# Attention scores of a graph kernel: the destination's row by a matmul on the edge tiles' own rows, and no look-ups or gathers of destinations

## The chip, the core and the metric

The kernel runs on 1 core of one Trainium2 chip. The metric is device time in microseconds (us) of one execution. PE is TensorE (PEld its weight load), DVE is VectorE, ACT is ScalarE, POOL is GpSimd, SP is SyncE, which here only issues DMAs.

## What is computed

Two graph blocks over 50,000 nodes of 128 numbers and 25,000 edges sorted by destination, in float32. The first block (ten graph convolutions) gives x1. The second is attention over the edges; the change touches the tables made for both and the scores of the second:

```python
q = (x @ Wq + bq).reshape(n, H, C)
k = (x @ Wk + bk).reshape(n, H, C)
v = (x @ Wv + bv).reshape(n, H, C)
e = (edge_attr @ We).reshape(-1, H, C)
kj = k[src] + e
vj = v[src] + e
alpha = jnp.einsum('ehc,ehc->eh', q[dst], kj) / np.sqrt(C)
```

For every edge this needs the row of x1 of its source (for k and v) and the row of x1 of its destination (for q).

## The kernel before

**Tiles.** The edges fill TE = 196 tiles of 128 (98 pairs of tiles). Odd tiles lie in reverse order. Nodes are placed in slots so that a node with incoming edges has its slot where the run of its edges ends (`lead` is 1 there): its "own" row lies in the same tile and partition as that edge. Other nodes fill the free slots. For every edge tile a 128 x 128 matrix says which edges have the same destination; a matmul with it (`sums_all`) adds up the messages, and `carry` takes a run across a tile's border.

**Stages, in order.** (1) `prepare`: degrees, positions, tables. (2) `local_pass`: all ten layers for nodes without incoming edges, PE bound; beside it DVE builds the same-destination matrices (`build`), POOL looks up tables of positions (`edge_tables`). (3) `coupled_stages`: ten stages over the 98 pairs, first, then (mid, end) four times (r = 0 to 3), last. POOL gathers source rows by indirect DMA. In the end stages of r = 1, 2, 3 POOL also looks up where each destination's row lies (`dst_pair`, 196 indirect DMAs; `found_here`). (4) `scores`, the stage of the change. (5) `shares_and_finish`: softmax, weighted sums, the closing layers, output.

**Scores before.** A pair j takes one of four buffers (s = j % 4) of what is loaded and one of two (s % 2) of most of what is computed. `skewed` writes an engine's program: at turn t it runs each body for pair t minus its lag, in the order of the list; unless `unrolled`, four turns stand in a loop on the engine. POOL (unrolled by a Python loop): four indirect gathers of 128 rows of 512 bytes from x1_tab, two by source, two by destination. SP: three copies of the pair's edge attributes (32 partitions x 1 KB each), and five pairs later the store of the values. PE at turn t: `turn`(t), four transposes into bank s % 2, then `multiply`(t - 1), 14 matmuls of the split (high and low part) product. ACT: `edge_high`(t), `copy`(t) of the transposed rows to their high part, `take`(t - 1) of values and query. DVE: `edge_low`(t), `low`(t), `weigh`(t - 1). The rings that order it: a gather of pair j waits for `turned`(j - 4), a load for `edge_low`(j - 4), `turn`(j) for `low`(j - 2), `take`(j) for the store of pair j - 4.

Of the kernel before, what the change touches and what calls it, by code (L numbers as in the profile page):

```python
# [31 lines left out]
P = 128  # L32
# [173 lines left out]
def gnn_kernel(nc, a, out):  # L206
# [3 lines left out]
    def sb(name, shape, dt=F32):  # L210
        return nc.alloc_sbuf_tensor(name, list(shape), dt)
# [22 lines left out]
    v_tab = dram("v_tab", [SLOTS, D])  # L234
    alpha_line = dram("alpha_line", [HEADS, SLOTS])
# [10 lines left out]
    dst_pair = sb("dst_pair", [P, TE, 2], I32)  # L246
# [11 lines left out]
    with ExitStack() as passing:  # L258
# [6 lines left out]
        early("up", [P, P])  # L265
        early("down", [P, P])
# [14 lines left out]
def prepare(nc, a, S, counts, m):  # L281
# [8 lines left out]
    with ctx:  # L290
        src_i, dst_i, dst_f, up, down, own_three = (m[n] for n in ("src_i", "dst_i", "dst_f", "up", "down", "own_three"))
# [59 lines left out]
        with nc.Block() as block:  # L351
            @block.sync
            def _(sp):
                sp.dma_start(dst_i[:], a["dst"]).then_inc(S["edges_in"], 16)
                sp.dma_start(next_i[:], a["dst_next"]).then_inc(S["edges_in"], 16)
                sp.dma_start(src_i[:], a["src"]).then_inc(S["edges_in"], 16)

            @block.gpsimd
            def _(pool):
                nc.gpsimd.memset(ones[:], 1.0).then_inc(S["filled"], 1)  # L360
# [10 lines left out]
                pool.wait_ge(S["filled"], 2)  # L371
                nc.gpsimd.affine_select(ident[:], ident[:], [[-1, P]], ALU.not_equal, 1.0, base=0,
                                        channel_multiplier=1).then_inc(S["masks"], 1)
                nc.gpsimd.affine_select(up[:], ones[:], [[1, P]], ALU.is_ge, 0.0, base=0,
                                        channel_multiplier=-1).then_inc(S["masks"], 1)
                nc.gpsimd.affine_select(down[:], ones[:], [[-1, P]], ALU.is_ge, 0.0, base=0,
# [3 lines left out]
                nc.gpsimd.memset(m["dst_pair"][:], 0)  # L380
# [8 lines left out]
            def _(dve):  # L389
# [6 lines left out]
                dve.wait_ge(S["masks"], 7)  # L396
# [59 lines left out]
        with nc.Block() as block:  # L456
# [171 lines left out]
            def _(sp):  # L628
                sp.wait_ge(S["rows_set"], 3)
                sp.wait_ge(S["masks"], 8)  # L630
# [5 lines left out]
                sp.wait_ge(S["edges_in"], 96)  # L636


def edge_tables(nc, a, S, m, pool, xo):
# [36 lines left out]
    pool.wait_ge(S["placed"], 32 * TE)  # L676
# [72 lines left out]
def local_pass(nc, a, S, counts, m):  # L749
# [21 lines left out]
    with ctx:  # L771
# [93 lines left out]
        with nc.Block() as block:  # L865
# [196 lines left out]
            def _(dve):  # L1062
# [79 lines left out]
                def build(b, q, odd):  # L1142
# [66 lines left out]
def coupled_stage(nc, S, counts, m, kind, r, source, target, others):  # L1209
# [46 lines left out]
    with nc.Block() as block:  # L1256
# [37 lines left out]
        def _(pool):  # L1294
            def gather(j, s):
# [9 lines left out]
                for t in found_here.get(j, ()):  # L1305
                    pool.indirect_dma_start(
                        out=m["dst_pair"][:, t, :], out_offset=None, in_=m["pos_tab"],
                        in_offset=bass.IndirectOffsetOnAxis(ap=m["dst_i"][:, t:t + 1], axis=0),
                        bounds_check=NPAD - 1, oob_is_err=False).then_inc(S["dst_found"], 16)
# [8 lines left out]
            found_here = {}  # L1318
            if end and r in (1, 2):
                found_here = {j: [(r - 1) * (pairs // 2) + j // 2] for j in range(1, pairs, 2)}  # L1320
            elif end and r == 3:
                found_here = {j: [pairs + j] for j in range(pairs)}
# [302 lines left out]
def scores(nc, a, S, counts, m):  # L1625
# [9 lines left out]
    ph = counts.phase(pairs, {"gathered*": 64, "own_in*": 48, "turned": 1, "copied": 1,  # L1635
# [6 lines left out]
    with ctx:  # L1642
        rows = sb("a_rows", [P, 4, 4, D])

# [18 lines left out]
        with nc.Block() as block:  # L1663
            @block.sync
            def _(sp):
# [25 lines left out]
                skewed(sp, pairs, [(0, load), (5, store)])  # L1691
# [5 lines left out]
            def _(pool):  # L1697
                nc.gpsimd.memset(m["neg_half"][:], -0.5).then_inc(S["a_constants"], 1)

                def gather(j, s):  # L1700
# [3 lines left out]
                    for n, which in enumerate((m["src_pair"], m["dst_pair"])):  # L1704
                        for i in range(2):
                            t = j * 2 + i
                            pool.indirect_dma_start(
                                out=rows[:, s, n * 2 + i, :], out_offset=None, in_=m["x1_tab"],
                                in_offset=bass.IndirectOffsetOnAxis(ap=which[:, t, 0:1], axis=0)
                            ).then_inc(S[f"gathered{s}"], 16)  # L1710
                pool.wait_ge(S["dst_found"], 16 * TE)
# [4 lines left out]
            def _(pe):  # L1716
                pe.wait_ge(S["a_split"], 5)

                def turn(j, s):
# [3 lines left out]
                    for i in range(4):  # L1723
                        last = nc.tensor.transpose(psum[s % 2][:, i * P:(i + 1) * P], rows[:, s, i, :], ident[:])
# [19 lines left out]
                skewed(pe, pairs, [(0, turn), (1, multiply)])  # L1744

            @block.scalar
            def _(act):
# [6 lines left out]
                def edge_high(j, s):  # L1754
                    act.wait_ge(S[f"own_in{s}"], ph.ring_at("own_in", j, s))
                    if past(j, 4):
                        act.wait_ge(S["product"], ph.at("product", j - 4))
                    nc.scalar.activation(edge_parts[0:3 * ED, s, :], edge[:, s, :], ACT.Copy).then_inc(S["edge_high"], 1)

                def take(j, s):  # L1760
# [11 lines left out]
                    last.then_inc(S["query"], 1)  # L1772
                act.wait_ge(S["a_weights"], 288)
                nc.scalar.activation(w_hi[:], m["w_kvq"][:], ACT.Copy).then_inc(S["a_high"], 1)
                nc.scalar.activation(w_edge_hi[:], w_edge[:], ACT.Copy).then_inc(S["a_high"], 1)
                skewed(act, pairs, [(0, edge_high), (0, copy), (1, take)])

            @block.vector
            def _(dve):
# [4 lines left out]
                dve.wait_ge(S["a_split"], 2)  # L1784
                v.tensor_scalar(not_rest[:], is_rest[:], -1.0, 1.0, ALU.mult, ALU.add).then_inc(S["a_split"], 1)
# [578 lines left out]
```

## Time and profile before

| | |
|---|---|
| time of 3 runs | median 7772.25 us (7767.53 to 7774.64) |
| the profiled execution's own time | 7764.07 us, of which 7762.0 us are its span |
| busy in the span | PE 81%, PEld 68%, DVE 78%, ACT 49%, POOL 67% |
| mean granted TensorE clock | 0.925 |
| moved by DMA | 1483 MB in 978,825 packets |

A row of the groups by line has the line, the engine, the operation, output <- inputs, the count, busy time with the mean of one in ns, and the idle time just before with what ended it. Line numbers are those of the kernel before.

### The profile page before, as it was taken

The numbers are of one execution on the slowest core, as the hardware profiler recorded it, in microseconds if no ns is written. First come the engines' busy times: TensorE is split into PE (matmuls) and PEld (weight loads), VectorE is DVE, ScalarE is ACT, GpSimd is POOL, SyncE is SP. The second block draws the span as 40 slices with busy tenths as digits, with TensorE's granted clock in tenths as the row PEclk, the third lists the DMA queues.
The fourth block names the chain that finished last, engine by engine and source line by source line (L and its number), as shares of the span: only waits on it lengthen the run. The fifth ranks groups of instructions, "written<-read, shape, count | busy, mean of one in ns | idle before, by whom it ended". The sixth has DMA issues, their size and how long they took to land. (4 is left out here: it accounts for less than half of the span.)

```text
span 7762.0 us, 157556 instructions
## 1 busy us (share of the span) xinstructions
PE 6300.4 (81%) x37064; PEld 5242.3 (68%) x37064; DVE 6057.8 (78%) x15597; ACT 3773.5 (49%) x10500; POOL 5188.7 (67%) x5858
## 2 busy tenths in 40 slices
PE   7689999999997569899988998899887655557776
PEld 3688898888887348677756776677565545555554
DVE  8678888788887768798888878887898863348887
ACT  6466666666665767435711571157222332234443
POOL 0588888878853768556766676667665656656665
PEclk8899999999998999999999999999999987778998
DMA  0355555554443658797789778977998642224332
GB/s 2 113 162 161 162 164 164 161 159 148 147 155 127 189 182 246 246 302 232 228 296 311 235 226 295 311 234 225 356 388 274 188 141 82 84 88 129 123 122 86
DMA packets 978825, 1483.35 MB, mean 191 GB/s; under 512 B 164277, under 2 KB 445177, under 8 KB 978223
## 3 DMA queue, kind: packets, MB, share of 16 engines
q1 hardware_dynamic: 670639, 909.34, 35.0%
q0 software_dynamic: 153920, 322.36, 15.9%
q10 hardware_dynamic: 153664, 244.12, 8.7%
q8 instruction: 319, 5.23, 0.3%
q14 instruction: 283, 2.32, 0.1%
HBM read 902.55 MB, written 573.01 MB: 190 GB/s over the span
## 5 line engine op out<-in xcount | busy, mean ns | idle before, releaser
L1339 PE MATMUL bank<-c_rows,sums_all 128*128 128x256 f32 (+1 forms) x3920 | 1317.9, 419 | 616.0 <-DVE c_rows L1490 283.5
L743 PE MATMUL bank<-wf_w,c_xt 128*128 128x256 f32 x6272 | 1618.2, 381 | 2.0 <-DVE y L1548 2.0
L1384 ACT ACTIVATE c_xt<-bank 128x512 f32<-128x512 f32 (+1 forms) x980 | 556.1, 567 | 1651.5 <-issue 759.3
L1339 PEld LDWEIGHTS bank<-c_rows,sums_all 128*128 128x128 f32 x3920 | 631.9, 193 | 1056.0 <-issue 499.7
L743 PEld LDWEIGHTS bank<-wf_w,c_xt 128*128 128x128 f32 x6272 | 1135.8, 191 | 127.6 <-ACT c_xt L1384 3.5
L1300 POOL DMA_INDIRECT c_rows<-t_tab,src_pair x784 | 857.7, 1094 | 536.1 <-PE bank L1339 366.5
L1490 DVE SCALAR_TENSOR_TENSOR c_rows<-bank,carry,c_rows 32x256 f32<-32x256 f32 (+1 forms) x1950 | 913.6, 468 | 340.6 <-PE bank L1339 109.6
L1300 POOL DMA_INDIRECT c_rows<-z_tab,src_pair x784 | 768.3, 980 | 291.6 <-issue 189.2
L1022 ACT ACTIVATE lx_hi<-bank 128x512 fp32r<-128x512 f32 (+1 forms) x1000 | 569.8, 572 | 589.1 <-PE bank L991 450.8
L1077 DVE TENSOR_TENSOR lx_lo<-bank,lx_hi 128x512 fp32r<-128x512 f32 (+1 forms) x1000 | 656.8, 657 | 233.0 <-ACT lx_hi L1022 189.8
L733 PE MATMUL bank<-wf_hi,lx_hi 128*128 128x256 f32 x3200 | 724.7, 309 | 76.6 <-issue 51.6
L1504 DVE SCALAR_TENSOR_TENSOR c_u<-bank,lead,c_own 128x256 f32<-128x256 f32 x1764 | 758.4, 467 | 0.4
L733 PE MATMUL bank<-wf_lo,lx_hi 128*128 128x256 f32 x3200 | 658.1, 288 | 0.0
L733 PE MATMUL bank<-wf_hi,lx_lo 128*128 128x256 f32 x3200 | 657.0, 288 | 0.0
L1416 ACT ACTIVATE c_squares<-y,c_root_deg 128x256 f32<-128x256 f32 x980 | 490.0, 501 | 341.6 <-issue 211.3
L1350 PE MATMUL bank<-ident,c_u 128*128 128x128 f32 x3724 | 576.4, 276 | 0.3 <-DVE c_u L1504 0.3
L733 PEld LDWEIGHTS bank<-wf_hi,lx_hi 128*128 128x128 f32 x3200 | 504.3, 196 | 96.7 <-issue 73.0
L1313 POOL TENSOR_TENSOR c_inv<-c_ss,c_neg_half 128x2 f32<-128x2 f32 x588 | 423.5, 720 | 199.6 <-DVE c_ss L1573 89.6
L1999 POOL DMA_INDIRECT out_dram<-fl_y,node_of x396 | 394.9, 997 | 241.8 <-DVE fl_y L2317 145.6
L1350 PEld LDWEIGHTS bank<-ident,c_u 128*128 128x128 f32 x3724 | 473.5, 143 | 93.1 <-issue 3.7
L733 PEld LDWEIGHTS bank<-wf_lo,lx_hi 128*128 128x128 f32 x3200 | 512.1, 196 | 0.0
L733 PEld LDWEIGHTS bank<-wf_hi,lx_lo 128*128 128x128 f32 x3200 | 507.5, 195 | 0.0
(329 smaller groups left out, 14992.6 us busy)
## 6 DMA issues: line engine op xcount, KB each, us to landing
c_z<-z_tab SPq DMA_DIRECT2D x882, 256.0 KB
z_tab<-lz SPq DMA_DIRECT2D x400, 256.0 KB
t_tab<-lt SPq DMA_DIRECT2D x400, 256.0 KB
z_tab<-y ACTq DMA_DIRECT2D x392, 256.0 KB
c_own<-z_tab SPq DMA_DIRECT2D x392, 256.0 KB
t_tab<-y ACTq DMA_DIRECT2D x392, 256.0 KB
c_own<-t_tab SPq DMA_DIRECT2D x392, 256.0 KB
fl_x<-x_tab SPq DMA_DIRECT2D x396, 128.0 KB
```

Source lines behind the costliest of these rows:

```text
L733: last = nc.tensor.matmul(out, x(k), w[:, k, :], start=(n == 0), stop=(n == 3 * ks - 1 and not bias))
L743: last = nc.tensor.matmul(out, x(k), w[:, k, :], start=(k == 0), stop=(k == ks - 1 and not bias))
L1022: nc.scalar.activation(x_hi[:, k].rearrange("p k n -> p (k n)")[:, 0:n], psum[k][:, 0:n], ACT.Copy).then_inc(S["high"], 1)
L1077: v.tensor_tensor(x_lo[:, k].rearrange("p k n -> p (k n)")[:, 0:n], psum[k][:, 0:n], x_hi[:, k].rearrange("p k n -> p (k n)")[:, 0:n].bitc ...
L1300: pool.indirect_dma_start(out=rows[:, s, i, 0:win], out_offset=None, in_=source, in_offset=bass.IndirectOffsetOnAxis(ap=m["src_i"][:, t:t ...
L1313: nc.gpsimd.tensor_tensor(inv[:, s, :], ss[:, s, :], m["c_neg_half"][:], ALU.pow).then_inc(S["inverted"], 1)
L1339: nc.tensor.matmul(psum[s % 2][:, i * win:(i + 1) * win], sums[:, j * 2 + i, :], rows[:, s, i, 0:win], start=True, stop=True).then_inc(S[" ...
L1350: last = nc.tensor.transpose(psum[2 + s % 2][:, k * H2 + i * P:k * H2 + (i + 1) * P], u[:, s % 2, i, k * P:(k + 1) * P], ident[:])
L1384: nc.scalar.activation(xt[:, s % 2].rearrange("p k n -> p (k n)")[:, 0:n], psum[2 + s % 2][:, 0:n], ACT.Copy).then_inc(S["copied"], 1)
L1416: last = nc.scalar.activation(m["c_squares"][:, i, :], y[:, s, i, :], ACT.Square, scale=m["c_root_deg"][:, bass.ds(j * 2 + i, 1)], accum_o ...
L1490: v.scalar_tensor_tensor(rows[p0:p0 + 32, s, i, 0:win], before, m["carry"][p0:p0 + 32, bass.ds(j * 2 + i, 1)], rows[p0:p0 + 32, s, i, 0:wi ...
L1504: last = v.scalar_tensor_tensor(u[:, s % 2, i, 0:win], psum[s % 2][:, i * win:(i + 1) * win], m["lead"][:, bass.ds(j * 2 + i, 1)], u[:, s ...
```

## The change

1. `sums_all` is no longer masked: `build` was a scalar_tensor_tensor with the masks `up` / `down`, and is a tensor_scalar; the two masks go from `prepare`.
2. The 196 look-ups of `dst_pair` in the end stages and the 196 gathers of destination rows in `scores` are dropped.
3. In their place `scores` loads, for each of a pair's two tiles, 127 of the tile's own rows of x1_tab (512 bytes each, every second row of the table) and one row more: of the last edge in the tile's order, from a small table `last_tab`. ACT scales them with `told` (1 where the row is the destination of a run, and at the last edge), and PE multiplies them with `sums_all`: that gives the transposed destination rows directly, two matmuls in place of two transposes.
4. `last_tab` is filled at the start of `scores`: two index loads in `prepare`, two look-ups at the end of `edge_tables`, two gathers, one copy; SP waits for it before its first load.
5. SP and PE are unrolled in `scores`; ACT runs `copy` and `take` one turn later; a load also waits for `turned`(j - 4).

```diff
@@ edge_tables, after the look-ups of the sources
+    for i in range(2):
+        pool.indirect_dma_start(out=m["last_pos"][:, i, :], out_offset=None, in_=m["pos_tab"],
+                                in_offset=at(m["last_dst"][:, i:i + 1]), bounds_check=NPAD - 1, oob_is_err=False
+                                ).then_inc(S["placed"], 16)
@@ local_pass, build
-                    ins = v.scalar_tensor_tensor(built[:, s, i, :], rows_f[:, s, i * P:(i + 1) * P],
-                                                 m["dst_f"][:, bass.ds(b * 8 + (n * 2 + i), 1)],
-                                                 m[("up", "down")[i % 2]][:], ALU.is_equal, ALU.mult)
+                    ins = v.tensor_scalar(built[:, s, i, :], rows_f[:, s, i * P:(i + 1) * P],
+                                          m["dst_f"][:, bass.ds(b * 8 + (n * 2 + i), 1)], None, ALU.is_equal)
@@ coupled_stage, POOL
-                for t in found_here.get(j, ()):
-                    pool.indirect_dma_start(
-                        out=m["dst_pair"][:, t, :], out_offset=None, in_=m["pos_tab"],
@@ scores, SP
+                sp.wait_ge(S["last_found"], 32)
+                sp.dma_start(m["last_tab"], last_rows[0:pairs, :, :]).then_inc(S["last_out"], 16)
+                sp.wait_ge(S["last_out"], 48)
                 def load(j, s):
                     if past(j, 4):
                         sp.wait_ge(S["edge_low"], ph.at("edge_low", j - 4))
+                        sp.wait_ge(S["turned"], ph.at("turned", j - 4))
+                    own = m["x1_tab"].rearrange("(j p i) c -> i p j c", p=P, i=2)
+                    for i, (rows_, row) in enumerate(((slice(0, P - 1), P - 1), (slice(1, P), 0))):
+                        sp.dma_start(ends[rows_, s, i:i + 1, :], own[i][rows_, bass.ds(j, 1), :]
+                                     ).then_inc(S[f"own_in{s}"], 16)
+                        sp.dma_start(ends[row:row + 1, s, i:i + 1, :],
+                                     m["last_tab"].rearrange("j i c -> i j c")[i:i + 1, bass.ds(j, 1), :]
+                                     ).then_inc(S[f"own_in{s}"], 16)
-                skewed(sp, pairs, [(0, load), (5, store)])
+                skewed(sp, pairs, [(0, load), (5, store)], unrolled=True)
@@ scores, POOL: two gathers a pair by src_pair in place of four; before them
+                for i in range(2):
+                    pool.indirect_dma_start(
+                        out=last_rows[:, i, :], out_offset=None, in_=m["x1_tab"],
+                        in_offset=bass.IndirectOffsetOnAxis(ap=m["last_pos"][:, i, 0:1], axis=0)
+                    ).then_inc(S["last_found"], 16)
@@ scores, PE, turn
-                    for i in range(4):
-                        last = nc.tensor.transpose(psum[s % 2][:, i * P:(i + 1) * P], rows[:, s, i, :], ident[:])
+                    for i in range(2):
+                        nc.tensor.transpose(psum[s % 2][:, i * P:(i + 1) * P], rows[:, s, i, :], ident[:])
+                    pe.wait_ge(S["edge_high"], ph.at("edge_high", j))
+                    for i in range(2):
+                        last = nc.tensor.matmul(psum[s % 2][:, (2 + i) * P:(3 + i) * P], ends[:, s, i, :],
+                                                m["sums_all"][:, j * 2 + i, :], start=True, stop=True)
-                skewed(pe, pairs, [(0, turn), (1, multiply)])
+                skewed(pe, pairs, [(0, turn), (1, multiply)], unrolled=True)
@@ scores, ACT, edge_high, and the order of the bodies
+                    for i in range(2):
+                        nc.scalar.activation(ends[:, s, i, :], ends[:, s, i, :], ACT.Copy,
+                                             scale=told[:, bass.ds(j * 2 + i, 1)])
-                skewed(act, pairs, [(0, edge_high), (0, copy), (1, take)])
+                skewed(act, pairs, [(0, edge_high), (1, copy), (2, take)])
```

## Rows read from the trace of the kernel before

**Rows 1.** Windows: end stages of r = 0, 1 and 3, then the scores.

```profile
core 0: us, PE busy (x) PEld busy (x) DVE busy (x) ACT busy (x) POOL busy (x), PEclk, DMA share, GB/s
...
3175.00:3550.00 375.00, 336.77 (x1571) 247.90 (x1571) 335.17 (x786) 109.54 (x197) 191.89 (x203) 0.96 0.87 281
...
3885.00:4330.00 445.00, 375.90 (x1675) 268.09 (x1676) 365.67 (x790) 58.53 (x98) 287.00 (x256) 0.96 0.89 296
...
5435.00:5915.00 480.00, 409.51 (x1755) 283.58 (x1755) 445.82 (x873) 109.01 (x196) 309.87 (x290) 0.97 1.02 372
...
6350.00:6944.00 594.00, 335.11 (x1764) 323.99 (x1764) 206.34 (x600) 149.44 (x590) 374.43 (x393) 0.71 0.28 82
```

**Rows 2.** Groups by line and form in the stretch of the scores.

```profile
L1707 POOL DMA_INDIRECT a_rows<-x_tab,dst_pair x196 | 188.9, 964 | 59.7 <-issue 59.7
L1707 POOL DMA_INDIRECT a_rows<-x_tab,src_pair x196 | 185.4, 946 | 144.0 <-remote 81.3 <-issue 45.7 <-PE bank L1724 16.8
...
L1724 PE MATMUL bank<-ident,a_rows 128*128 128x128 f32 x392 | 82.3, 348 | 25.8 <-DVE a_w_edge_parts L1798 24.6 <-issue 0.6 <-DMA a_rows<-x_tab,dst_pair 0.6
...
L1770 ACT ACTIVATE a_q<-bank 128x128 f32<-128x128 f32 x196 | 45.3, 299 | 0.0
```

**Rows 3.** ACT's timeline in the scores: two starts after idle time (start, us).

```profile
6592.11 0.45 ACT L1765 ACTIVATE a_v<-bank 128x128 f32<-128x128 f32 x2 [9.65 <-remote]
6603.85 0.45 ACT L1765 ACTIVATE a_v<-bank 128x128 f32<-128x128 f32 x2 [8.74 <-remote]
```

**Rows 4.** Waits in 6400 to 6900 us, summed: us, times, longest.

```profile
ACT a_v L1765 <- remote: 308.5, 35, 10.8
```

**Rows 5.** DMA queues in 231 to 234 us: packets, MB, share of 16 engines.

```profile
q1 hardware_dynamic: 675, 0.67, 71.3%
```

**Rows 6.** SP's timeline just before: three copies of 99 partitions each.

```profile
229.42 0.36 SPq L632 DMA_DIRECT2D pos_tab<-pos_rows  x1
...
230.26 1.02 SPq L634 DMA_DIRECT2D own_tab<-late_rows  x1
```

**Rows 7.** DMA queues in 2500 to 2800 us (first coupled stage).

```profile
q1 hardware_dynamic: 47585, 22.94, 26.8%
```

**Rows 8.** DMA queues in 6400 to 6900 us (scores).

```profile
q0 software_dynamic: 10848, 22.24, 15.3%
q1 hardware_dynamic: 24048, 19.16, 12.7%
```

**Rows 9.** SP's timeline where its program is unrolled (last stage).

```profile
7199.85 0.43 SPq L1974 DMA_DIRECT2D fl_x<-x_tab  x1
7200.32 0.43 SPq L1968 DMA_DIRECT2D fl_x<-x_tab  x1
```

**Rows 10.** PE in the first coupled stage, by form: matmul with `sums_all`.

```profile
L1339 PE MATMUL bank<-c_rows,sums_all 128*128 128x128 f32 x392 | 98.4, 334 | 151.8 <-DVE c_rows L1490 123.0 <-issue 28.7
```

**Rows 11.** Timeline at the start of the scores.

```profile
6351.32 1.02 POOL L1707 DMA_INDIRECT a_rows<-x_tab,src_pair  x1 [0.60 <-issue]
...
6358.40 7.14 SPq L1685 DMA_DIRECT2D a_edge<-in_edge_attr  x14
...
6361.38 0.42 ACT L1758 ACTIVATE a_edge_parts<-a_edge 96x256 fp32r<-96x256 f32 x1 [0.26 <-DMA a_edge<-in_edge_attr]
```

**Rows 12.** SP's timeline at the end of the scores.

```profile
6926.19 1.24 SPq L1685 DMA_DIRECT2D a_edge<-in_edge_attr  x3
```

**Rows 13.** The look-ups: ns min/median/max, first and last start.

```profile
L1306 POOL DMA_INDIRECT dst_pair<-pos_tab,dst_i x196: 1002/1007/1213, 3889.4 to 5891.7; - x196
```

**Rows 14.** Waits in 5440 to 5910 us (end stage of r = 3).

```profile
POOL c_rows L1300 <- PE bank L1339: 82.6, 88, 2.1
```

**Rows 15.** `lbuilt` in the local pass: ns min/median/max.

```profile
L1158 DVE SCALAR_TENSOR_TENSOR lbuilt<-lrows_i,dst_f,up x98: 319/344/364, 253.7 to 2351.1; 128x128 f32<-128x128 f32 x98
```

**Rows 16.** Window in the local pass, columns as in rows 1.

```profile
300.00:2200.00 1900.00, 1727.15 (x13749) 1678.03 (x13750) 1531.47 (x2995) 1245.23 (x3623) 1523.03 (x1982) 0.95 0.53 158
```

**Rows 17.** Timeline of the kernel's first microseconds: DVE's first work.

```profile
5.53 1.21 DVE L398 CAST dst_f<-dst_i 128x196 f32<-128x196 int32 x1 [5.53 <-POOL above L378]
```

More of the change, by code:

```diff
@@ L234, in gnn_kernel @@
     v_tab = dram("v_tab", [SLOTS, D])
+    last_tab = dram("last_tab", [TE // 2, 2, D])
     alpha_line = dram("alpha_line", [HEADS, SLOTS])
@@ L356, in _ @@
                 sp.dma_start(src_i[:], a["src"]).then_inc(S["edges_in"], 16)
+                sp.wait_ge(S["filled"], 1)
+                for i, row in enumerate((P - 1, 0)):
+                    sp.dma_start(m["last_dst"][0:TE // 2, i:i + 1],
+                                 a["dst"][row:row + 1, :].rearrange("o (j i) -> i j o", i=2)[i],
+                                 allow_slow_non_contiguous=True).then_inc(S["last_out"], 16)
             @block.gpsimd
             def _(pool):
+                nc.gpsimd.memset(m["last_dst"][:], 0).then_inc(S["filled"], 1)
                 nc.gpsimd.memset(ones[:], 1.0).then_inc(S["filled"], 1)
@@ L1317, in _ @@
                 pool.wait_ge(S["c_constants"], 1)
[L1318 to L1322, printed above, removed]
             for j in range(pairs + (8 if rooted else 0)):
@@ L1634, in scores @@
     v, psum, ident = nc.vector, m["psum"], m["ident"]
-    ph = counts.phase(pairs, {"gathered*": 64, "own_in*": 48, "turned": 1, "copied": 1,
+    ph = counts.phase(pairs, {"gathered*": 32, "own_in*": 112, "turned": 1, "copied": 1,
                               "product": 1, "query": 1, "values": 1, "weighed": 1, "alpha": 1, "stored*": 16,
@@ L1642, in scores @@
     with ctx:
-        rows = sb("a_rows", [P, 4, 4, D])
+        rows = sb("a_rows", [P, 4, 2, D])
+        ends = sb("a_ends", [P, 4, 2, D])
+        last_rows = sb("a_last_rows", [P, 2, D])
+        told = sb("a_told", [P, TE])
         K = 3 * ED + 2
@@ L1703, in gather @@
                         pool_wait(pool, S[f"gathered{s}"], ph.ring_at("gathered", j, s, back=1), S["apart"])
[L1704 to L1711, printed above, removed]
+                    for i in range(2):
+                        t = j * 2 + i
+                        pool.indirect_dma_start(
+                            out=rows[:, s, i, :], out_offset=None, in_=m["x1_tab"],
+                            in_offset=bass.IndirectOffsetOnAxis(ap=m["src_pair"][:, t, 0:1], axis=0)
+                        ).then_inc(S[f"gathered{s}"], 16)
+                for i in range(2):
+                    pool.indirect_dma_start(
+                        out=last_rows[:, i, :], out_offset=None, in_=m["x1_tab"],
+                        in_offset=bass.IndirectOffsetOnAxis(ap=m["last_pos"][:, i, 0:1], axis=0)
+                    ).then_inc(S["last_found"], 16)
                 for j in range(pairs):
@@ L1755, in edge_high @@
                     act.wait_ge(S[f"own_in{s}"], ph.ring_at("own_in", j, s))
+                    for i in range(2):
+                        nc.scalar.activation(ends[:, s, i, :], ends[:, s, i, :], ACT.Copy,
+                                             scale=told[:, bass.ds(j * 2 + i, 1)])
                     if past(j, 4):
@@ L1784, in _ @@
                 dve.wait_ge(S["a_split"], 2)
+                for i, row in enumerate((P - 1, 0)):
+                    v.tensor_scalar(told[:].rearrange("p (j i) -> p j i", i=2)[:, :, i],
+                                    m["lead"][:].rearrange("p (j i) -> p j i", i=2)[:, :, i],
+                                    ident[:, row:row + 1], None, ALU.max)
                 v.tensor_scalar(not_rest[:], is_rest[:], -1.0, 1.0, ALU.mult, ALU.add).then_inc(S["a_split"], 1)
```

26 lines of the change are left out of this document (11 added, 15 removed).

## The prediction

> **What bounds the kernel now.** I read the table of windows by stage first, since the kernel is a row of stages with different limits, and then only the stages that the change touches. In the end stages DVE is busy 82 to 93% of the time and PE 84 to 90%, and the DMA engines up to 1.02 of their time, above one because services on an engine overlap a little [rows 1]. The scores are another world: 594 us for 98 pairs, 6.06 us a pair, with PE busy 56%, POOL 63%, DVE 35%, the clock at 0.71 and the DMA engines at 0.28 [rows 1]. No engine is full.
>
> The groups by line say why POOL is not: 392 gathers of 0.95 us with 0.3 us between them are 5.0 us a pair, and it stands 81 us for something that is not an engine's recorded end [rows 2]. ACT's timeline shows the beat: it starts once in 12 us, after 9 to 10 us of idle time, and then does two pairs at once [rows 3]; 35 such waits are 308 of 500 us [rows 4]. So the stage goes in steps of two pairs: PE does two products, ACT, DVE and PE wait for one another through rings of two, and POOL's gathers hang on `turned` of four pairs back. The profile doesn't name the cause of the long waits; any load that takes under about 6 us a pair is hidden in that beat, and one that takes more becomes the bound.
>
> **The loads of own rows.** This is the term that decides. A pair gets two copies of 127 partitions with one run of 512 bytes each, on SP's queue. The question is on how many of the 16 DMA engines such a copy runs. The nearest rows are three copies of 99 partitions, issued within 0.9 us with nothing beside them [rows 6]: while they run, 16 engines are busy 71.3% [rows 5], that is 11.4 engines; 99 is 9 x 11, and 11 of 16 would be 69%, where 15 engines (seven rows each) would be 94%. So the copy was dealt out in equal shares to the largest number of engines that divides its partitions. 127 is a prime number. By that reading (an estimate: no copy of a prime number of rows is in the trace) all 127 rows go to one engine, for both copies of every pair.
>
> The Trainium skill, page "DMA: Bandwidth & Descriptors", section "Why a DMA increments its semaphore by 16 and not by 1", says that for a DMA from SP or ACT the count of engines is the largest one up to 16 that divides the slowest dimension of both sides, gives 127 partitions as a case of one engine, and puts it on the lowest-numbered engines; the row of 99 agrees with it (11 engines), no row shows 127. It also tells of an exception, for some copies from POOL, where 127 partitions are shared out over all 16; by that the stage would be the first rival below, some 7600 us for the kernel; by the rule for SP it is the sum that follows.
>
> Price of a row: in the first coupled stage SP's queue moves almost only 512-byte runs: 47,585 packets and 22.94 MB in 300 us at 26.8% of 16 engines [rows 7], 0.268 x 300 x 16 / 47,585 = 27.0 ns a packet; if the few 4-byte packets in it cost nothing, 22.94 MB are 44,800 rows of 28.7 ns. I take 28 ns. Two copies are 254 rows x 28 ns = 7.11 us a pair on one engine.
>
> That engine has its share of the rest too. In 500 us (82.5 pairs) of the scores SP's queue took 12.7% of every engine and POOL's 15.3% [rows 8]: 0.77 us a pair for edges and stores, which stay, and 0.93 us for four gathers, of which half stay, 0.46 us. The two single rows and semaphore writes are some 0.04 us. Sum: 7.11 + 0.77 + 0.46 + 0.04 = 8.38 us a pair. The other 15 engines have 1.3 us.
>
> Is this engine kept fed? Loads run up to four pairs ahead (they wait for `turned` and `edge_low` of j - 4), and the store of j - 5, behind which the next load is queued on SP, waits for values that ACT writes one load's landing later. So two to three loads, 16 to 25 us of its work, lie in the ring while ACT, PE, ACT, DVE and PE pass a pair on in less; even a late beat of 12 us is covered. Stores stand in the same ring, but `take` wants that of four pairs back, which lands with load j + 5 and before the load that ACT awaits anyway. PE's new wait, for `edge_high`(j) and so for load j, has `multiply`(j - 1) behind it: product, values and store of a pair come one load later, which the rings allow. So the engine sets the pace.
>
> **The rest of the scores** lies under 8.38 us a pair. SP: eight issues of 0.47 us when unrolled [rows 9], 3.8 us. POOL: two gathers, 2.5 us. PE: two transposes of 348 ns [rows 2] become two matmuls of 334 ns [rows 10], nothing to 0.1 us on 3.4 us (335 us / 98). ACT: two scalings of 0.30 us, priced by `a_q` of the same size [rows 2], 0.6 on 1.5 us. The unrolling costs instruction loads and takes away loop branches; both lie beside the engine's work. If the engine were not the bound, SP's 3.8 us and PE's 3.4 to 3.8 us would be next.
>
> **Start and end of the stage.** The first load was issued at 6358.4, after 18 weight copies; its data were used at 6361.38 [rows 11]. POOL starts its gathers at 6351.32, so the two gathers of last rows are done when SP comes to `last_tab`; its copy and the wait for it cost one such landing, 2.5 to 3 us. The engine starts at about 6361. The last edges were issued at 6926.2 to 6927.4 [rows 12] and the stage ended at 6944, 17 us later; of that I put 14 us behind the last landing. Stage end: 6361 + 98 x 8.38 (821) + 14 = 7196, against 6944: +252 us. Overlap of services, at least the 2% of the 1.02 row, takes off 16 us: +236.
>
> **The parts outside.** The look-ups: 196 x 1.3 us of POOL's time [rows 13], but in the stage that has the most of them (r = 3, 98) POOL stood 83 us for PE in 88 waits [rows 14], so they are hidden; the work they were hidden by is the chain of DVE and PE through `carried`. Their small packets, where the engines are full, may be worth 4 us. Bounds: 0 and, if every look-up delayed a gather on the chain, all 255 us, which POOL's waits for PE exclude; I keep 0 to -15. `build`: 344 ns [rows 15] to some 270 ns of a one-input operation, 196 x 0.07 = 14 us of DVE, in a stage where PE is busy 1727 of 1900 us [rows 16]: nothing. Masks: DVE's first work waits for POOL's selects at 5.53 [rows 17]; two fewer and a memset more are -0.4 us. Two look-ups at the end of the local pass lie under it.
>
> Sum: +236 - 4 = +232 us on the profiled execution's 7764 us, 7996; the median of the runs is 8 us above that execution: **8004 us, say 8005**.
>
> **Rivals.**
> - *The copies are spread over 15 or 16 engines and the beat of two pairs goes, with PE and SP unrolled.* For it: nothing in the trace has a prime number of rows, and the loads would be 1.7 us a pair. Then SP (3.8 us) and PE set the pace, some 4.1 us a pair: 98 x 4.1 + 25 = 427 us for the stage, -167: 7600 us. Against it: the 71.3% row. This is the other side; it decides as soon as the copies use four engines or more (254 x 28 / 4 = 1.8 us). Chance 0.10.
> - *Spread, but the beat stays.* Its 12 us for two pairs gain at most four scalings of 0.3 us in the chain: 6.06 to 6.7 us a pair, 7770 to 7830 us. Chance 0.04.
> - *One engine, but slower for one ring alone.* The copies of 99 rows, of 1 KB, paid 0.713 x 3 x 16 / 675 = 51 ns a packet; if a lone ring pays that for half the bytes, a pair is 12.9 + 1.3 = 14.2 us and the kernel some 8590 us. Against it: those copies were of double size, and at the same bytes per ns 512 bytes cost 26 ns. Chance 0.08.
> - *The forecast*, one engine at 27.0 to 28.7 ns: chance 0.78. Its own range: with 27.0 ns and all other traffic overlapped, 98 x 6.86 = 672 us, +103: 7875; with 28.7 ns and no overlap, 98 x 8.56 = 839 us, +270: 8042.
>
> **Numbers.** The range takes in the forecast's own range nearly whole and goes on to 8150 for a ring that is slowed in part by the gathers beside it or runs dry at times: 7880 to 8150, about 8 in 10. A change under 0.2% (16 us) can't be told from none. Slower: 0.78 + 0.08 + half of the second rival, 0.88; same 0.02; faster 0.10.
>
> **What would show it.** In the profile after: scores of 800 to 850 us; the DMA share there near (8.4 + 15 x 1.3) / (16 x 8.4) = 0.2; ACT's idle time ended by the DMA of `a_ends` once a pair, every 8.3 us, in place of 9 us once in two pairs; 254 rows a pair in 512-byte packets; POOL waiting for `turned`; end stages within a few us of before. It is wrong if the DMA share in the scores stays at 0.25 or above with less time (spread), if the packets of 512 bytes take 50 ns (third rival), or if idle time in the scores ends at DVE or PE and not at a load.

## The result, and the profile after

The changed kernel takes 7841.8 us (median of 4 runs, 7838.2 to 7855.1), the kernel before beside it 7773.4 us: ratio 1.0091 [1.0079, 1.0103]. It is slower, by 68 us where 232 were forecast, and the time lies below the range. The profiled execution took 7855.1 us, the slowest of the four.

The windows of the changed kernel, each from POOL's first gather of a stage to that of the next (the scores to the first scatter of the output): local pass, end stages of r = 1, 2, 3, scores.

```profile
core 0: us, PE busy (x) PEld busy (x) DVE busy (x) ACT busy (x) POOL busy (x), PEclk, DMA share, GB/s
250.10:2494.90 2244.80, 2009.13 (x16000) 1951.48 (x16000) 1777.08 (x3495) 1446.88 (x4200) 1667.54 (x2189) 0.95 0.52 153
3903.80:4306.60 402.80, 368.61 (x1666) 265.93 (x1666) 362.84 (x784) 58.52 (x98) 234.25 (x197) 0.97 0.94 320
4647.80:5051.10 403.30, 368.33 (x1666) 265.84 (x1666) 362.80 (x784) 58.53 (x98) 234.18 (x196) 0.97 0.93 320
5392.40:5876.00 483.60, 407.79 (x1764) 282.16 (x1764) 450.88 (x881) 109.45 (x196) 216.02 (x196) 0.98 1.01 373
6309.60:7062.20 752.60, 504.75 (x2027) 435.36 (x2027) 217.12 (x623) 222.94 (x814) 188.43 (x198) 0.55 0.25 70
```

By the same marks the three end stages took 432.0, 435.3 and 493.0 us in the kernel before and the scores 621.0 us (the windows of [rows 1] have other bounds). So the scores are longer, and the end stages are shorter with the same work on DVE. The waits of the changed kernel from 6500 to 6900 us (us, times, longest) answer to [rows 4]:

```profile
ACT a_ends L1775 <- DMA a_edge<-in_edge_attr: 284.2, 56, 6.4
DVE a_x_lo L1829 <- ACT a_x_hi L1770: 280.7, 55, 6.4
POOL a_rows L1717 <- PE bank L1741: 274.3, 55, 6.3
```

Fifty-six waits in 400 us: 7.14 us a pair, and each ends with the last load of the pair (edges stand behind the own rows in the same queue). ACT's and SP's timeline shows one pair, in place of the double step of [rows 3]:

```profile
6604.17 0.25 SPq L1690 DMA_DIRECT2D a_ends<-x_tab  x1
6604.25 0.69 ACT L1775 ACTIVATE a_ends<-a_ends,a_told 128x128 f32<-128x128 f32 x2 [5.14 <-DMA a_edge<-in_edge_attr]
6604.46 2.64 SPq L1692 DMA_DIRECT2D a_ends<-last_tab  x1
...
6607.14 1.36 SPq L1696 DMA_DIRECT2D a_edge<-in_edge_attr  x3
...
6608.55 0.42 SPq L1701 DMA_DIRECT2D v_tab<-a_v  x1
6609.07 0.24 SPq L1690 DMA_DIRECT2D a_ends<-x_tab  x1
6609.35 1.64 SPq L1692 DMA_DIRECT2D a_ends<-last_tab  x1
6611.03 0.25 SPq L1690 DMA_DIRECT2D a_ends<-x_tab  x1
6611.16 0.69 ACT L1775 ACTIVATE a_ends<-a_ends,a_told 128x128 f32<-128x128 f32 x2 [4.78 <-DMA a_edge<-in_edge_attr]
```

SP issues without a pause too: here the issue of a copy of one row takes 1.6 to 2.6 us behind one of 127 rows. Is SP then the bound, or does it only wait because the engine's queue of waiting rows (its ring) takes no more? The first group of experiments asks that.

### The profile page after: what moved, and what is told of

It is laid out like the page before. It is cut to its first block and busy times, and to the rows that moved or that the text cites. A ratio compares the mean times of both kernels' runs of the same rounds, so it can differ in the third digit from the quotient of the medians.

```text
span 7852.9 us, 157304 instructions
## 1 busy us (share of the span) xinstructions
PE 6458.1 (82%) x37260; PEld 5356.6 (68%) x37260; DVE 6051.1 (77%) x15599; ACT 3830.1 (49%) x10696; POOL 4839.1 (62%) x5469
```

## Experiments

Eighteen runs were made in five groups, each group on a chip of its own and at its own time, with the kernel before beside them. The kernel before took 7730 us in the first group, 7777 in the second, 7599, 7597 and 7596 in the others; what lies behind that difference is part of the question. `rows101`, `rows61`, `half_rows`, `before_two_gathers`, `before_act_lag`, `pool_work`, `before_again` and `before_third` are one execution each, the others the median of 4 to 10. Stage lengths in us, from the same marks as above:

| kernel (group) | local pass | end r = 1 | r = 2 | r = 3 | scores |
|---|---|---|---|---|---|
| before_again (2) | 2225.6 | 436.8 | 433.6 | 492.6 | 623.7 |
| after_again (2) | 2238.1 | 403.1 | 401.5 | 483.3 | 745.4 |
| before_third (4) | 2216.8 | 402.2 | 404.0 | 485.7 | 534.9 |
| after_third (4) | 2233.6 | 403.2 | 403.1 | 485.2 | 743.8 |
| split (1) | 2242.4 | 401.0 | 402.9 | 485.5 | 469.2 |
| wide (1) | 2240.7 | 402.8 | 401.6 | 484.2 | 371.5 |
| lookups_back (1) | 2238.5 | 419.1 | 421.4 | 495.7 | 764.0 |
| before_no_lookups (1) | 2221.4 | 403.6 | 404.5 | 483.2 | 614.7 |
| before_build (2) | 2238.5 | 435.3 | 435.8 | 493.7 | 622.9 |
| before_both_unrolled (2) | 2225.7 | 439.9 | 438.2 | 493.4 | 617.9 |
| rows101 (3) | 2233.3 | 403.4 | 403.2 | 485.1 | 626.5 |
| rows61 (3) | 2231.2 | 401.7 | 403.8 | 485.3 | 427.7 |
| half_rows (3) | 2234.1 | 402.8 | 402.9 | 486.7 | 585.0 |
| wide_stt (3) | 2217.0 | 401.6 | 403.8 | 485.2 | 348.1 |
| before_two_gathers (4) | 2214.6 | 403.0 | 403.5 | 485.8 | 307.8 |
| before_act_lag (4) | 2216.8 | 403.5 | 404.0 | 484.2 | 534.6 |
| pool_work (5) | 2233.7 | 403.2 | 403.1 | 485.6 | 764.5 |
| wide_stt_again (5) | 2217.3 | 402.9 | 403.4 | 484.0 | 345.1 |

### Is it one DMA engine?

`split` cuts a copy of 127 rows in two:

```diff
-                        sp.dma_start(ends[rows_, s, i:i + 1, :], own[i][rows_, bass.ds(j, 1), :]
+                        for lo, hi in parts_:   # 0:112, 112:127; or 1:113, 113:128
+                            sp.dma_start(ends[lo:hi, s, i:i + 1, :], own[i][lo:hi, bass.ds(j, 1), :]
```

> The changed kernel, but each copy of 127 own rows issued as one of 112 rows and one of 15. Nothing is left out. Theory 1: the stage's pace of 7.14 us a pair is one DMA engine's work on 254 rows (23.5 ns each) and 1.2 us more. With 112 = 16 x 7 and 15 = 15 x 1 rows the copies lie on 16 and 15 engines, 0.4 us a pair, and the next bound is SP with ten issues of 0.43 us or PE with 3.4 to 3.8: 4.3 to 4.6 us a pair in the scores, kernel at 7842 - 98 x 2.7 = 7580 us (7540 to 7640). Theory 2: the pace is that of SP's issues or of the waits between engines: two issues more, so 7.1 us a pair or more, kernel at 7842 us or more. Theory 3: the engine's work is one bound, but below it the beat of two pairs of the kernel before comes back, 6.06 us a pair: 7736 us.

Measured: 7566.4 us, ratio 0.9786 [0.9769, 0.9802]. The same rows by two issues more on SP cost 276 us less in the scores than in `after_again`: by the starts of ACT's `take` a pair now goes in 4.3 us, as theory 1 expected. So neither SP's count of issues nor the waits between engines set the pace of 7.14 us: it was how the 127 rows of a copy were dealt out. The issue of a copy of one row, 2.29 us (median) in the changed kernel, takes 0.25 us here, so SP's long issues were a wait behind the rows and not SP's own work.

`wide` loads partitions 1 to 126 of both tiles by one copy with 1 KB runs, and partitions 0 and 127 from a table that holds one own row and the last edge's row for each:

```diff
+                    sp.dma_start(run(ends[1:P - 1, s, :, :]), pair_rows(m["x1_tab"], j)[1:P - 1]
+                                 ).then_inc(S[f"own_in{s}"], 16)
+                    sp.dma_start(run(ends[0:P:P - 1, s, :, :]),
+                                 m["last_tab"].rearrange("j h i c -> h j (i c)")[:, bass.ds(j, 1), :]
+                                 ).then_inc(S[f"own_in{s}"], 16)
```

> The changed kernel, but a pair's own rows come by one copy of 126 partitions with 1 KB each (both tiles of partitions 1 to 126) and one of two rows of 1 KB (partitions 0 and 127, from a small table that holds for these partitions one own row and the last edge's row). Nothing is left out. Seven loads a pair become five. Theory 1: 126 = 14 x 9 rows on 14 engines, 9 x 40 ns a pair; SP has six issues, 2.6 us, POOL 2.5, so PE at 3.4 to 3.8 us or ACT sets the pace, 3.8 to 4.2 us a pair: kernel at 7842 - 98 x 3.1 = 7538 us (7500 to 7580). Theory 2 (waits between the engines, whatever the loads): 7842 us. Theory 3 (beat of 6.06 us): 7736 us.

Measured: 7455.4 us, ratio 0.9643 [0.9627, 0.9659], 83 us below what was expected and below its range: 3.3 us a pair. Its window of the scores:

```profile
6304.70:6676.20 371.50, 298.24 (x2027) 276.21 (x2027) 220.10 (x623) 221.88 (x814) 187.91 (x197) 0.87 0.50 142
```

PE is busy 80% of it, at a granted clock of 0.87, where in the changed kernel, with PE busy 67%, the clock was 0.55. The share of the DMA engines is twice as high (0.50 against 0.25) in half the time.

### What does a row cost?

`rows101` and `rows61` shorten the copies to other prime numbers of rows, `half_rows` cuts each row to 256 bytes. In all three the partitions or halves not loaded hold zeros.

```diff
-                    for i, (rows_, row) in enumerate(((slice(0, P - 1), P - 1), (slice(1, P), 0))):
+                    ... slice(0, 101), slice(1, 102)     # rows101
+                    ... slice(0, 61), slice(1, 62)       # rows61
+                    ... [..., 0:D // 2] on both sides    # half_rows
```

> The changed kernel with copies of 101 own rows (a prime number) in place of 127; the other 26 partitions keep zeros, so part of the queries is computed from zeros. Theory 1 (one engine, a fixed price for each row of 512 bytes in its unbroken stream): 52 rows a pair fewer at 23.5 ns are 1.22 us a pair less, scores at 5.9 us a pair, stage 745 - 120 = 625 us. If the price is the 28 ns that the prediction took, 1.46 us a pair less: 602 us. Theory 2 (101 rows spread over more engines, or the pace not the rows'): stage under 480 us, or unchanged at 745 us.

> The changed kernel with copies of 61 own rows (a prime number) in place of 127; the other partitions keep zeros. Theory 1: 122 rows x 23.5 ns + 1.2 us are 4.0 us a pair, below or at what the kernel with copies of 112 and 15 rows shows as the next bound (4.5 us a pair with ten issues on SP, here eight), so 4.0 to 4.4 us a pair, stage 415 to 460 us. Theory 2: SP's blocking behind the single-row copies has a part of its own in the pace: more than 4.6 us a pair.

> The changed kernel with the copies of 127 rows cut to the first 64 numbers of each row (256 bytes); the other half keeps zeros. Theory D (price per descriptor): 23.5 ns a row as before, scores at 7.1 us a pair, stage about 745 us. Theory B (price per byte): 11.8 ns a row, 254 rows are 3.0 us, and 4.2 us a pair with the rest: stage some 440 us. Between the two: a fixed part and a part for the bytes.

`rows101`: 626.5 us. Against 743.8 to 745.4 us, 52 rows a pair less are worth 1.20 to 1.21 us, 23.0 to 23.3 ns a row, as theory 1 expected; the forecast's 28 ns would have given 602. `rows61`: 427.7 us, within what was expected; the slope there, (626.5 - 427.7) / 98 / 80, is 25 ns. `half_rows`: 585.0 us, between the two theories; by the stage a row costs (743.8 - 585.0) / 98 / 254 = 6.4 ns less.

The stage's length understates what the bytes cost. In the packet records of `half_rows` the 256-byte packets start 14.3 ns apart within a run of them, 9.3 ns less than the 23.6 ns of the changed kernel's packets. But 254 of them are 3.6 us of the 5.5 us that a pair takes there, and the rest, 1.9 us, is more than the 1.1 us that stand beside the rows in the changed kernel. What fills it was not followed. By the distance of the starts most of a 512-byte row's price goes with its bytes: 18.6 of 23.6 ns, an estimate from the two distances.

In the packet records of the changed kernel's scores the 512-byte packets last 27.2 ns each, but start 23.6 ns apart. The 27 to 28.7 ns that the prediction read as busy time over packets [rows 7] was right as busy time; services overlap, and a queue's pace is the distance of the starts. The Trainium skill, page "DMA: Bandwidth & Descriptors", section "Why small descriptors are slow (HBM only)", gives a fixed cost of about three cycles a packet beside one for each 32 bytes; with the page's 850 MHz that is an estimate of 22.4 ns for 512 bytes and 12.9 ns for 256. The measured 23.6 ns lie 6% above the first and the 14.3 ns 11% above the second, and the page would have priced the term better than the row did.

### The end stages: do look-ups cost?

`lookups_back` puts the 196 look-ups back into the changed kernel, their result unused. `before_no_lookups` takes them from the kernel before, whose gathers of destination rows go by the sources' positions (so the queries come from other rows).

> The changed kernel with the 196 look-ups of dst_pair put back into the end stages of r = 1, 2, 3; their result is not used. Theory A: the look-ups delayed gathers on the chain of DVE and PE, and dropping them gave the 29, 32 and 10 us by which these three stages are shorter: kernel at 7842 + 71 = 7913 us (7895 to 7925), the three stages at 432, 435 and 493 us again. Theory B: they were hidden, as the prediction said, and the stages are shorter for another part of the change (matrices without masks, other memory places): 7842 us, 0 to 15 more.

> The kernel before without the 196 look-ups of dst_pair; the gathers of destination rows in the scores go by the source's positions instead, so the query is computed from wrong rows. Theory A (look-ups cost 71 us in the end stages): 7773 - 71 = 7702 us, scores at 6.06 us a pair as before. Theory B (hidden): 7773 us, 0 to 15 less.

Measured: 7900.7 us, ratio 1.0219 [1.0202, 1.0236], and 7689.4 us, ratio 0.9949 [0.9932, 0.9965]. The end stages follow the look-ups: 419, 421 and 496 us with them, some 403, 403 and 484 without. Theory A, then, but in this group the three stages give some 46 us and not 71, and the kernel before is itself 44 us faster. That 7900.7 us lie in theory A's range is partly luck: 19 us of it stand in the scores (764.0 us, see the last section). So both kernels ran again on one chip:

> The kernel before, unchanged, to have its trace on the same chip as the next three. All theories: end stages of r = 1, 2, 3 at 432, 435, 493 us, local pass 2228 us, scores 621 us. If the look-ups' price differs from chip to chip (the two kernels that asked for it gave 46 us added to the changed one and 40 us off the one before, where the first traces gave 71), the end stages here are 415 to 425 us.

> The changed kernel, unchanged, for its trace beside that of the kernel before on one chip. End stages of r = 1, 2, 3 at 403, 403, 484 us, local pass 2245 us if its 17 us more are an effect of the change and 2228 if they are an accident of one execution, scores 753 us. Ratio to the kernel before 1.009.

Ratio of `after_again` 1.0089 [1.0072, 1.0106]; `before_again` took 7773.7 us. With look-ups 437, 434, 493 us, without 403, 402, 483: 75 us. And a third time, after a group (3) in which the kernel before took under 7600 us:

> The kernel before, unchanged, for its trace on the chip of this group. Where a chip runs it faster than 7777 us, theory A puts the difference in the look-ups (end stages of r = 1 and 2 under 432 us) and in the scores (stage under 621 us); theory B spreads it over all stages by the same share.

> The changed kernel, unchanged, on the same chip. Its scores are one DMA engine's work, so they take 745 to 753 us on any chip, and its end stages 403, 403 and 484 us. On a chip where the kernel before takes 7777 us the ratio is 1.009, where that takes 7599 us it is about 1.03.

Here the change costs 231 us: 7827.7 us, ratio 1.0306 [1.0289, 1.0323]. The changed kernel takes nearly the same time in both groups; the kernel before does not. Its look-ups cost nothing here (402, 404, 486 us) and its scores take 535 us. Theory A of `before_third` holds for most of it: of the 177 us between its span here and in `before_again`, 64 lie in the end stages of r = 1 and 2 and 89 in the scores; 9 lie in the local pass and 7 in the end stage of r = 3. The windows of `before_again`, end stage of r = 1 and scores:

```profile
3881.20:4318.00 436.80, 372.94 (x1666) 267.79 (x1666) 362.88 (x784) 58.51 (x98) 278.22 (x245) 0.97 0.89 296
...
6357.10:6980.80 623.70, 354.64 (x1831) 338.86 (x1831) 220.14 (x627) 162.70 (x618) 371.92 (x394) 0.70 0.30 84
```

and of `before_third`:

```profile
3868.70:4270.90 402.20, 366.65 (x1666) 265.22 (x1666) 362.94 (x784) 58.51 (x98) 276.53 (x246) 0.98 0.94 321
...
6271.90:6806.80 534.90, 376.20 (x1831) 355.27 (x1831) 223.48 (x628) 176.57 (x618) 376.49 (x393) 0.65 0.35 98
```

In the end stage the same instructions have the same busy time within 2%, and the gaps differ. In the scores PE and ACT are even busier in the shorter stage (PE by 22 us, at the lower clock), so there too the gaps make the difference. The waits name them. In the end stage of r = 1, `before_again`:

```profile
ACT c_xt L1384 <- remote: 164.4, 31, 6.5
...
DVE c_rows L1490 <- remote: 23.2, 25, 1.2
```

None of the waits of `before_third` there is put down to "remote", and none of `before_no_lookups` in group 1. "Remote" means that the semaphore's record stands where no engine's recorded end comes shortly before it and no DMA answers to it. The timeline of the scores shows such a wait. In `before_again` a product's last matmul (L1741) starts at 6515.26, the next product's at 6518.18; ACT, which waits for the first of them, starts at 6520.86, 5.2 us after its end:

```profile
6515.26 0.41 PE L1741 MATMUL bank<-a_w_hi,a_x_lo 128*128 128x128 f32 x1
...
6518.18 0.28 PE L1741 MATMUL bank<-a_w_hi,a_x_lo 128*128 128x128 f32 x1
6518.30 0.63 PE L1724 MATMUL bank<-ident,a_rows 128*128 128x128 f32 x4
6520.86 0.45 ACT L1765 ACTIVATE a_v<-bank 128x128 f32<-128x128 f32 x2 [8.85 <-remote]
```

In `before_third` ACT starts 0.12 us after that end, and POOL issues one gather after the other:

```profile
6504.62 0.42 PE L1741 MATMUL bank<-a_w_hi,a_x_lo 128*128 128x128 f32 x1
6504.70 0.94 POOL L1707 DMA_INDIRECT a_rows<-x_tab,src_pair  x1 [0.30 <-issue]
6505.16 0.45 ACT L1765 ACTIVATE a_v<-bank 128x128 f32<-128x128 f32 x2 [2.58 <-PE bank L1741]
```

`take` waits for the store of four pairs back as well, but in `before_again` that one had landed at 6499.54, long before. PE's own semaphore is what comes late: it should go up at the recorded ends 6515.68 and 6518.46, and those of the transposes at 6516.55 and 6518.93; all four records stand together, between 6520.76 and 6521.02. In the scores of `before_third` all 98 records of the products stand within 15 ns of the recorded end, and so they do in those of `after_again`, on the chip of `before_again`.

So in groups 1 and 2, and in the forecast's own profile, signals of PE reach the others microseconds late in these stages, and in group 4 they don't. In the end stages it goes with the look-ups: in that of r = 1, 165 us of ACT's waits end in "remote" in the kernel before (forecast's profile), none in `before_no_lookups`, and 111 us again in `lookups_back`. The cause was not found. The traces hold a hint that reaches further: those of groups 1 and 2 and of the first two kernels have a record for only 63 to 66% of the semaphore updates that the program's own instructions make (17,583 of 27,749 in `before_again`), those of groups 3 to 5 have all of them. So late signals and missing records occur in the same groups, and some of what a trace of these groups calls "issue" or "remote" may be a missing record. Whether the chip, its state at that time or the recording itself is behind both, no run tells: no chip was used for two groups.

One run was meant to tell POOL's time from the look-ups' DMAs: the look-ups replaced by 1.3 us of fills on POOL, without a DMA.

> The changed kernel with 1.3 us of other work on POOL (three fills of 0.42 us, each waited for) in each of the 196 places where the kernel before had a look-up; no DMA is added. On a chip where the kernel before takes 7730 to 7777 us: theory A (the look-ups cost by POOL's time) gives end stages of r = 1 and 2 of 419 to 435 us in place of 403; theory B (they cost by their DMAs or by what these do to other signals) leaves them at 403. On a chip where the kernel before takes 7600 us both give 403 us, and the run tells nothing.

It fell to a chip where the kernel before takes 7596 us. It took 7847.4 us, with the three stages at 403, 403 and 486 us, which by the expectation tells nothing.

### The beat of the scores

`before_both_unrolled` unrolls SP's and PE's programs of the kernel before. `before_two_gathers` drops the gathers of destination rows (PE transposes the source rows twice, so the queries come from them). `before_act_lag` gives ACT the changed kernel's order.

> The kernel before with the programs of SP and PE in the scores unrolled; nothing is left out. Theory A: the beat of two pairs (6.06 us a pair) is made by the loops of SP or PE, so it goes: POOL's four gathers, 5.0 to 5.2 us a pair, set the pace, scores 98 x 1.0 us shorter, -100 us (-60 to -120). Theory B: the beat comes of the four gathers and the rings, whatever the loops: 0, at most 10 us either way.

> The kernel before with only the two gathers by source in the scores; PE transposes their rows twice, so the query is computed from wrong rows. Theory A: the four gathers a pair on POOL (5.0 us of issue with the gaps) and their landing make the pace and the beat: scores at 3.6 to 4.4 us a pair, stage 380 to 455 us. Theory B: the beat is made by the rings, the loops or ACT's order, whatever POOL has to do: 6.0 us a pair, stage 610 to 625 us.

> The kernel before with ACT's steps copy and take one turn later in the scores, as the change has them; nothing is left out. Theory A (the beat hangs on the gathers): stage within 10 us of 621. Theory B (ACT's order makes it, since its copy of a pair stands behind a load's wait): POOL's 5.0 to 5.2 us a pair, stage 515 to 535 us.

The loops don't make the beat: 617.9 against 623.7 us in the group that has it, ratio 0.9991 [0.9981, 1.0000]. The other two fell to group 4, where the beat is missing. Without the two gathers the stage takes 307.8 us in place of 534.9, less than even theory A expected: there the four gathers set the pace of 5.05 us a pair, 1.25 us each on POOL. ACT's order changes nothing (534.6 us). That this number lies in theory B's range is no sign for theory B, since the kernel before takes 534.9 there too; for the beat both runs are silent. What makes it, beyond the late signals that stand in its waits, stays open. In all, in this group, the change trades 227 us of gathers that it takes away for 436 us of loads on one engine; `wide_stt_again` takes 37 us more than `before_two_gathers` for the same rows.

### The local pass

It is 12 to 17 us longer in the changed kernel in each of the three pairs of traces (2244.8 against 2228.0 us in the first). `before_build` changes only the instruction that builds the matrices; `wide_stt` is `wide` with the old instruction, multiplying by a matrix of ones:

```diff
-                    ins = v.tensor_scalar(built..., rows_f..., m["dst_f"]..., None, ALU.is_equal)
+                    ins = v.scalar_tensor_tensor(built..., rows_f..., m["dst_f"]..., m["ones"][:], ALU.is_equal, ALU.mult)
```

> The kernel before with the matrices built by tensor_scalar without masks (the two masks are still made); nothing is left out. Theory A: this form, shorter by itself (278 against 342 ns in the traces), slows the local pass, by what it does to other engines' work: local pass 2245 us, kernel +17 us (+8 to +20). Theory B: the longer local pass of the changed kernel comes from its two look-ups at the end, the index loads or other memory places: kernel within 5 us. Theory C: freed time of DVE shortens the pass: up to 14 us less.

> The kernel with own rows in runs of 1 KB (126 and 2 partitions), and the same-destination matrices built by a scalar_tensor_tensor that multiplies with a matrix of ones: the same matrices, in the form of the kernel before. Nothing is left out. Theory A (the tensor_scalar form costs the local pass its 13 us): local pass at 2225 to 2228 us, kernel at ratio 0.9643 - 0.0016 = 0.9627 to the kernel before. Theory B (another part of the change lengthens the local pass): local pass at 2240 us, ratio 0.9643.

> The kernel with own rows in runs of 1 KB and the matrices built by scalar_tensor_tensor, as before, nothing left out. On a chip where the kernel before takes 7597 us: 7414 us again, ratio 0.976. On one where that takes 7777 us: the end stages are 403 us on every chip without look-ups, and the scores are 348 us on the faster kind of chip and 372 us with the copies in the same form on the slower kind, so 7414 + 24 = 7438 us, some 7435 to 7455, ratio 0.956 to 0.959. If late signals hold the scores up here too as they held those of the kernel before, the stage is over 400 us.

`before_build`: 7789.7 us, ratio 1.0019 [1.0010, 1.0029], local pass 2238.5 against 2225.6 us. `wide_stt`: 7414.4 us, ratio 0.9762 [0.9748, 0.9775], its local pass 2217.0 against 2231 to 2234 us of the three kernels beside it. The ratio of 0.9627 that was expected missed because the kernel before took 7599 us in this group and not 7730. `wide_stt_again`: 7414.5 us, 0.9761 [0.9744, 0.9777], again in a group where the kernel before takes under 7600 us, so what was expected for a chip where it takes 7777 us was not tested. The new form of the instruction is shorter, 279 ns in place of 343, and POOL's operations beside it are longer. In `before_again`, 300 to 2200 us, by line:

```profile
L889 POOL TENSOR_SCALAR lss<-lss 128x2 f32<-128x2 f32 x433 | 107.9, 249 | 92.9 <-ACT lsquares L1055 82.3 <-issue 0.5
```

and its wait behind POOL

```profile
ACT lt L1045 <- POOL linv L897: 144.7, 82, 3.6
```

are in `before_build`

```profile
L889 POOL TENSOR_SCALAR lss<-lss 128x2 f32<-128x2 f32 x430 | 119.9, 279 | 88.1 <-ACT lsquares L1055 76.4 <-issue 0.9
```

```profile
ACT lt L1045 <- POOL linv L897: 161.2, 83, 4.4
```

ACT waits 16 us more for POOL. In group 4, whose traces have all records, the same wait is 167.7 us in `before_third` and 188.7 us in `after_third`, and POOL's operation takes 249 and 280 ns. The Trainium skill, page "SBUF — State Buffer", section "SBUF: two separate sides", says that VectorE in a two-port mode locks GpSimd out of a shared port for the whole instruction; the builds run in 279 ns with a longest of 550 and POOL's small operations grow by 30 ns, which fits. But the same sentence of the page names an operation with two SBUF inputs beside it, which the old form is, so the page alone doesn't say why the new form costs POOL more, and no run here separates the port from POOL's other work.

## Why the prediction was wrong

| us | predicted | group 2 | group 4 |
|---|---|---|---|
| scores | +236 | +121.7 | +208.9 |
| look-ups, three end stages | -4 | -75.1 | -0.4 |
| local pass | 0 | +12.5 | +16.8 |
| all else | 0 | +3.3 | +2.7 |
| span | +232 | +62.4 | +228.0 |

- **The copies run on one engine** (the deciding term): right. `split`, `rows101` and `rows61` show it, and with it the way in which 99 partitions were read as 11 engines.
- **28 ns a row**: the first step that failed. It took the packets' busy time for their pace. 23.6 ns over 254 rows and 98 pairs are 110 us less, and the stage came out 112 us under the forecast (621 + 236 = 857 against 745). The other 1.27 us a pair nearly held: 7.14 less 254 x 23.6 ns is 1.15.
- **The look-ups hidden**: the second. POOL's waits for PE were read in the stage of r = 3, which lost only 9 us; the stages of r = 1 and 2 lost 32 to 34 each. In all that is 75 us, outside the bound of 15. In group 4, without late signals, they are hidden (0.4 us).
- **`build` at nothing**: mis-sized by 12 to 17 us. DVE's freed time and PE's busy share were asked, and not what the other form does to POOL, behind which ACT waits.
- 232 - 110 - 71 + 12.5 = 64 us in group 2, where 62 were measured. The range reaches 125 us below the forecast: the first two errors together go beyond it, neither does alone.
- **The beat**: that the loads would replace it as the bound was right. The prediction couldn't know that it comes and goes. In group 4 it is missing, the kernel before is 177 us faster and the change costs 3.06%. That this is near the forecast's 3.0% is luck: the stage after came out 113 us under the forecast (857 against 744) and the stage before 86 us under what it started from (621 against 535), and the local pass added 17.
- **The rivals**: the copies on more engines is what `split` and `wide` made true: `split` is 164 us faster than the kernel before beside it, where 172 were worked out (7772 to 7600). A lone ring at 51 ns a row is refuted by the 23.6 ns.
- **What would show it**: the DMA of the loads ends ACT's wait once a pair (every 7.1 us, not 8.3), and POOL waits for `turned`, as said. The share of the DMA engines is 0.25 where 0.2 was forecast; the sign against the forecast asked for 0.25 with less time, and the time is longer. Two signs failed: the stage took under 800 us, and the end stages moved by 75 us and not by a few.

## What to carry to other kernels

The copies from SP of 127, 101 and 61 rows, all prime numbers, ran at the pace of one DMA engine (127 is the trap that "all but one" sets). Copies of 112 and 15 rows, or of 126 rows of 1 KB with the odd rows from a small side table, brought the pair from 7.1 to 4.3 and 3.3 us. Price a queue by the distance of its packets' starts, not by their busy time. Before the cost of a small term is put at nothing, read its cover in every stage where it stands, and look at the other engines that work beside it. Where waits end in something that the profile can't name, expect that they may be gone on another chip or another day, and measure both kernels side by side again before the difference between them is trusted.

## What the runs showed of the hardware that was not expected

- The kernel before takes 7596 to 7777 us in different groups. Between groups 2 and 4 most of the difference lies where waits end late: in the end stages of r = 1 and 2 (34.6 and 29.6 us) and in the scores (89 us). The changed kernel, without the look-ups and with half the gathers in the scores, hardly shows it: it took 7842 and 7828 us. Where the signals are late, the trace also lacks about a third of the records of semaphore updates. The cause of both is open.
- The scores take 764 us in `lookups_back` and `pool_work`, 744 to 745 in the changed kernel. Both hold a table of 1568 bytes a partition more in front of the stage's buffers, and their 512-byte packets start 24.3 ns apart, not 23.6; 0.7 ns over 254 rows and 98 pairs are 17 us. Both also have the look-ups, or the fills in their place, in the stages before. That the place of a buffer matters to the engine is a guess; it was not tried apart.
